# A gated cross-attention and feed-forward block on one core: the weight signs issued by ScalarE a quarter later, all values loaded ahead of the probabilities

## The reference, cut to what matters

```python
# B=4, S=512, D=1024, 64 context rows per batch, 32 query heads, 8 key/value heads, head size 128
def reference(x, ctx, mask, g_xattn, g_ffn, wq, wk, wv, wo, weight, bias, gate_w, in_scale, out_scale):
    x = x + tanh(g_xattn) * attention(layernorm(x), ctx)      # RoPE on q and k, softmax, @ wo
    h = layernorm(x).reshape(-1, 1024)
    r = softmax(h @ gate_w.T)                                 # 8 experts
    f = (h * (r @ in_scale)) @ sign(weight).T * (r @ out_scale) + bias
    return x + tanh(g_ffn) * f.reshape(x.shape)
```

## Time and profile before

| | |
|---|---|
| median of 3 runs | 1574.86 us (1572.97 to 1578.59) |
| the profiled execution | 1577.78 us |
| its span, first to last instruction | 1576.0 us |
| PE / DVE / POOL / ACT busy | 95% / 65% / 46% / 39% of the span |
| mean granted clock of PE | 0.98 |
| moved by DMA | 192.42 MB, mean 122 GB/s |

### The profile page before, as it was taken

One profiled execution on the slowest core, in us unless ns is written; L12 is line 12 of the kernel. 1 busy time (PEld: TensorE's weight loads), 2 busy tenths in 40 slices (PEclk: granted clock), 3 DMA queues, 4 the chain that ended last, 5 costly groups with the idle time before them and its releaser, 6 DMA issues. The chain is left out here.

```text
span 1576.0 us, 26125 instructions
## 1 busy us (share of the span) xinstructions
PE 1489.4 (95%) x8720; PEld 1311.5 (83%) x8720; DVE 1031.2 (65%) x2370; ACT 614.3 (39%) x1183; POOL 720.9 (46%) x586
## 2 busy tenths in 40 slices
PE   6889999999999999999999379999878999999998
PEld 5878888888888888888888279999878999987887
DVE  6737887888878888788887635455344554756553
ACT  5722222222222222222222155556555555644442
POOL 6735554555545555455554333333223333325554
PEclk9999999999999999999999689999999999999999
DMA  7832122221222212222121694444995433542221
GB/s 275 274 100 54 41 74 79 73 69 40 73 77 74 69 40 73 75 75 70 40 67 49 207 384 152 121 128 133 347 349 197 128 100 100 156 160 110 104 80 67
DMA packets 93296, 192.42 MB, mean 122 GB/s; under 512 B 9232, under 2 KB 34320, under 8 KB 93072
## 3 DMA queue, kind: packets, MB, share of 16 engines
q1 hardware_dynamic: 89344, 188.13, 37.1%
q10 hardware_dynamic: 3888, 3.48, 0.6%
HBM read 133.90 MB, written 57.67 MB: 122 GB/s over the span
## 5 line engine op out<-in xcount | busy, mean ns | idle before, releaser
L51 PE MATMUL q_ps<-x_hi,w_hi 128*128 128x512 f32 x1024 | 399.6, 390 | 3.9 <-PEq L66 3.9
L53 PE MATMUL q_ps<-x_hi,w_lo 128*128 128x512 f32 x1024 | 400.6, 391 | 0.0
L52 PE MATMUL q_ps<-x_lo,w_hi 128*128 128x512 f32 x1024 | 400.0, 391 | 0.0
L1370 DVE TENSOR_TENSOR vw_lo<-bank,vw_hi 64x256 fp32r<-64x256 f32 x512 | 215.8, 422 | 244.7 <-ACT vw_hi L1173 239.4
L1327 POOL TENSOR_TENSOR w_lo<-w_raw,w_hi 128x512 fp32r<-128x512 f32 x128 | 164.8, 1288 | 324.7 <-ACT w_hi L1165 324.7
L1026 PE MATMUL bank<-vw_hi,x_hi 128*128 128x256 f32 x1024 | 291.2, 284 | 1.4 <-DVE last_rows L1380 1.4
L1027 PE MATMUL bank<-vw_lo,x_hi 128*128 128x256 f32 x1024 | 290.4, 284 | 0.0
L1028 PE MATMUL bank<-vw_hi,x_lo 128*128 128x256 f32 x1024 | 289.9, 283 | 0.0
L595 POOL TENSOR_TENSOR q_lo<-rot,q_hi 128x512 fp32r<-128x512 f32 x128 | 165.1, 1294 | 190.4 <-ACT q_hi L561 190.3
L1173 ACT CAST vw_hi<-bank 64x256 fp32r<-64x256 f32 x512 | 188.0, 367 | 158.9 <-PE bank L53 153.8
L51 PEld LDWEIGHTS q_ps<-x_hi,w_hi 128*128 128x128 f32 x1024 | 192.7, 188 | 45.4 <-issue 4.1
(11 more groups left out here) (129 smaller groups left out, 2466.8 us busy)
## 6 DMA issues: line engine op xcount, KB each, us to landing
w_raw<-in_wo SPq DMA_DIRECT2D x128, 256.0 KB, 2.7
w_raw<-in_wq SPq DMA_DIRECT2D x32, 512.0 KB, 5.2
probs_scratch<-pt_hi SPq DMA_DIRECT2D x64, 256.0 KB, 2.5
probs_scratch<-pt_lo SPq DMA_DIRECT2D x64, 256.0 KB, 3.2
x_hi<-probs_scratch SPq DMA_DIRECT2D x32, 512.0 KB, 8.3
x_lo<-probs_scratch SPq DMA_DIRECT2D x32, 512.0 KB, 9.5
x_in<-in_x SPq DMA_DIRECT2D x16, 512.0 KB, 4.6
last_rows<-in_x SPq DMA_DIRECT2D x8, 1024.0 KB, 6.9
```

What stands on the lines that cost most here:

```text
L51: pe.matmul(out, hi, rhs_hi, start=first, stop=False, **kw)
L52: pe.matmul(out, hi, rhs_lo, start=False, stop=False, **kw)
L53: return pe.matmul(out, lo, rhs_hi, start=False, stop=last, **kw)
L1370: done = nc.vector.tensor_tensor(vw_lo[at], vw_ps[hp % VW_BANKS][b * SK:(b + 1) * SK, h, :], vw_hi[at].bitcast(F32), ALU.subtract)
```

## The change

The change has two parts.

First, in SP's stream at the start of `finish`, the values of all eight groups are loaded ahead of the first piece of probabilities; before, groups 4 to 7 were loaded between pieces of probabilities, the last ahead of piece 12.

Second, loads and stores of the signs are taken out of SP's stream and issued by ACT: blocks 0 and 1 are loaded in ACT's step 14 of quarter (0, 3), and the steps of quarter (1, 0) take the signs, store them, and load the next blocks. Even steps take a sign and load, odd steps store. Quarter (1, 0) is written out and no longer part of a loop, and the load of the first rows of the next phase (with its wait for the signs) moves to step 0 of quarter (1, 3).

```diff
--- before.py
+++ after.py
@@ over_quarters
             quarter(0, NQ - 1, (1, 0))
-            with eng.Fori(0, NQ - 1) as q:
+            quarter(1, 0, (1, 1))
+            with eng.Fori(1, NQ - 1) as q:
                 quarter(1, q, (1, q + 1))
             quarter(1, NQ - 1, None)
@@ SP
-            def load_sign_raw(k):
-                wait(sp, sign_stored[k % 2], 16 * (k // 2))
-                sp.dma_start(rows[:, k % 2], a["weight_t"][k * P:(k + 1) * P, :]).then_inc(sign_raw_in[k % 2], 16)
-
-            def store_sign(k):
-                sp.wait_ge(sign_ready, k + 1)
-                sp.dma_start(scratch["signs"][k], rows[:, k % 2]).then_inc(sign_stored[k % 2], 16)
-
-            def signs(at):
-
-                if at in (4, 6):
-                    load_sign_raw((at - 4) // 2)
-                elif 9 <= at < 9 + 2 * (KT - 2):
-                    k = (at - 9) // 2
-                    if at % 2 == 1:
-                        store_sign(k)
-                    else:
-                        load_sign_raw(k + 2)
...
@@ SP, quarter
-                    if signs_from is not None:
-                        signs(signs_from + hp)
+                    if last and hp == 0:
+                        for i in range(2):
+                            sp.wait_ge(sign_stored[i], 16 * KT // 2)
+                        sp.dma_start(x1[0], rows_block(scratch["x1"], 0)).then_inc(x1_in[0], 16)
...
-            load_values(0)
-            sp.dma_start(gate_x[:], a["g_xattn"]).then_inc(gate_in, 16)
-            sp.dma_start(gate_f[:], a["g_ffn"]).then_inc(gate_in, 16)
+            for g in range(HKV):
+                load_values(g)
+                if g == 0:
+                    sp.dma_start(gate_x[:], a["g_xattn"]).then_inc(gate_in, 16)
+                    sp.dma_start(gate_f[:], a["g_ffn"]).then_inc(gate_in, 16)
             for hp in range(HP):
-                if hp % 2 == 0 and hp // 2 + 1 < HKV:
-                    load_values(hp // 2 + 1)
...
-            quarter(0, NQ - 1, (0, NQ - 2), probs_of={hp + LAG: hp for hp in range(HP - LAG)}, signs_from=0)
-            quarter(1, 0, (0, NQ - 1), probs_of={hp - HP + LAG: hp for hp in range(HP - LAG, HP)}, signs_from=HP)
-            sp.wait_ge(x1_stored, 16 * NQ)
-            for i in range(2):
-                sp.wait_ge(sign_stored[i], 16 * KT // 2)
-            sp.dma_start(x1[0], rows_block(scratch["x1"], 0)).then_inc(x1_in[0], 16)
+            quarter(0, NQ - 1, (0, NQ - 2), probs_of={hp + LAG: hp for hp in range(HP - LAG)})
+            quarter(1, 0, (0, NQ - 1), probs_of={hp - HP + LAG: hp for hp in range(HP - LAG, HP)})
@@ ACT
+            def load_sign_raw(k):
+                wait(act, sign_stored[k % 2], 16 * (k // 2))
+                act.dma_start(rows[:, k % 2], a["weight_t"][k * P:(k + 1) * P, :]).then_inc(sign_raw_in[k % 2], 16)
+
+            def store_sign(k):
+                act.wait_ge(sign_ready, k + 1)
+                act.dma_start(scratch["signs"][k], rows[:, k % 2]).then_inc(sign_stored[k % 2], 16)
+
+            def signs(at):
+
+                if at == 0:
+                    load_sign_raw(0)
+                    load_sign_raw(1)
+                elif at % 2 == 0 and at <= 2 * KT:
+                    sign(at // 2 - 1)
+                    if at >= 4 and at // 2 < KT:
+                        load_sign_raw(at // 2)
+                elif at % 2 == 1 and 3 <= at <= 2 * KT + 1:
+                    store_sign((at - 3) // 2)
@@ ACT, quarter
-                    if pair == 0 and isinstance(q, int) and q == NQ - 1 and hp % 2 == 1:
-                        sign(hp // 2)
+                    if pair == 0 and isinstance(q, int) and q == NQ - 1 and hp == HP - 2:
+                        signs(0)
+                    if pair == 1 and isinstance(q, int) and q == 0:
+                        signs(2 + hp)
```

More of the change, by code:

```diff
@@ L894, in store_x1, with quarter @@
                 sp.dma_start(own_quarter(scratch["x1"], pair, q), x_q).then_inc(x1_stored, 16)
-            def load_sign_raw(k):
-                wait(sp, sign_stored[k % 2], 16 * (k // 2))
-                sp.dma_start(rows[:, k % 2], a["weight_t"][k * P:(k + 1) * P, :]).then_inc(sign_raw_in[k % 2], 16)
-            def store_sign(k):
-                sp.wait_ge(sign_ready, k + 1)
-                sp.dma_start(scratch["signs"][k], rows[:, k % 2]).then_inc(sign_stored[k % 2], 16)
-            def signs(at):
-                if at in (4, 6):
-                    load_sign_raw((at - 4) // 2)
-                elif 9 <= at < 9 + 2 * (KT - 2):
-                    k = (at - 9) // 2
-                    if at % 2 == 1:
-                        store_sign(k)
-                    else:
-                        load_sign_raw(k + 2)
[L914 to L917, removed]
             STORE_AT, LOAD_AT = 7, 11
-            def quarter(pair, q, earlier, probs_of=None, signs_from=None, last=False):
+            def quarter(pair, q, earlier, probs_of=None, last=False):
                 for hp in range(HP):
```

## The result

The changed kernel takes 1547.32 us (median of 4 runs, 1545.35 to 1548.59) against 1573.91 us for the kernel before (4 runs): a ratio of 0.9824, 95% interval 0.9801 to 0.9848, or 26.6 us less. The forecast was 1543.6 us, 31.3 us less, with a range of 1538 to 1560; the time lies in the range, 0.3 us above the band 1541 to 1547 that had most of the chances. Four runs of the kernel before are in this median, where the forecast had three and stood on 1574.86. The profiled execution took 1548.2 us with a span of 1546.4; from the profiled execution before (1577.78) the forecast had come to 1546.5.

What follows compares the result with a forecast made beforehand. PE was taken to be held by late values in (0, 0) and by SP's waits for sign stores around (0, 3). 8.2 - 0.7 + 24.8 - 1.0 = 31.3 us off 1574.86 gave 1543.6 us, range 1538 to 1560.

Steps and rivals of the forecast that it cites:

- What bounds the kernel: PE's waits in (0, 0), for the values, and from (0, 3) into (1, 0), where quarters lose 24.8 us.
- Signs out of SP's queue: Quarters (0, 3) and (1, 0): SP loses 16 DMAs and their waits, and the 24.8 us go whole.
- PE's lead over a late piece of wo: Quarter (0, 3): 16.5 us of lead, into which a landing of 4.7 us and 5.7 us of backlog fit.
- The reason given for it: Quarters (0, 3) and (1, 0): SP's waiting for sign stores is what is lost; 8 MB also move to a freer quarter.
- The bytes as a rival: Quarter (0, 3): mixed reads and writes limited to 347 GB/s; up to 12.4 us lost, 1556 us; chance 0.09.
- The same on ACT: Quarter (1, 0): ACT issues signs and waits for stores landing in 4 to 5 us; costs PE 1 us.
- the 5 that I had named as the limit: Sign of being right: ACT's waits for `rows` or for a store sum to less than 5 us.
- Values first: Quarter (0, 0): PE's wait and half-rate clock go, 8.2 us, less 0.7 for delayed pieces: net 7.5 us.
- The delay of what follows: Quarter (0, 0): pieces of wo behind the values come later, so PE slips by 0 to 1 us, taken as 0.7.
- values in the way: Rival, quarter (0, 0): early wo later than allowed, or PE trades waits; first part worth 0 to 4.5, 1547 to 1551; chance 0.14.
- Slower: Rival, quarter (1, 0): stores on ACT's queue land after 13.0 us; 9.6 us slower, 1584 us; chance 0.03.
- ACT at 9.2 us: Rival, quarter (1, 0): stores land after 9.2 us on ACT's queue too; 19.1 us lost, 1562 us; chance 0.06.

Runs made afterwards that it cites:

- The cross: Four kernels, values as before: signs in SP's queue, quarter (0, 3) 1574.2 us (kernel before), (1, 0) 1554.0; signs issued by ACT, (0, 3) 1564.7, (1, 0) 1551.9.
- the second profile: The changed kernel run again without any edit, for another profile and more times: 1547.13 us, ratio 0.9829 to the kernel before.

## Why the prediction was right, and what was off

*What bounds the kernel.* Right. All of the gain comes from the two places named; the other quarters of the changed kernel from (0, 1) to (1, 2) stay at 56.9 to 57.1 us, (1, 3) at 62.5 (before 62.4), and the part after the quarters takes 169.0 us (before 168.7).

*Signs out of SP's queue: 24.8 us.* The size is right: 23.0 us in the profiles (138.9 to 115.9), 22.2 in the times of this part alone. PE's lead over a late piece of wo, worked out as 16.5 us, held: with landings of up to 12.3 us (0, 3) runs at full rate, with landings of up to 18.8, median 16.7 (signs by ACT in the old quarter), it does not. The engines carried 397 to 404 GB/s, above the 384 taken from the earlier trace rows, so the backlog was smaller than thought. That writing out a quarter costs nothing was right, too (57.07 and 57.06 us with the signs six steps later).

*The reason given for it* was half right. "What the rows show to be lost is SP's waiting" is contradicted: with the signs in SP's queue a quarter later, SP waits 35.9 us instead of 34.8 and PE loses 1.4 us; with the signs by ACT in the old quarter SP waits for none and 13.7 us stay lost. What the move removes is 8.4 MB from a quarter that is already full, and a wait that only costs in such a quarter. That the 24.8 us came out nearly whole is luck as far as the reason goes: the change moves both the quarter and the queue, so its time could not tell them apart. The cross shows most of the gain to be the quarter's; the queue's share is 9.5 us where the engines are full and within the spread of the runs where they are not. The Trainium skill's "Issuing engines are not separate DMA queues" ("DMA: Bandwidth & Descriptors") says that a second issuer brings no bandwidth. The traces agree: at most 408 GB/s with both issuing at full engines, 404 with SP alone. The 9.5 us of the queue are not against it: before, the engines moved only 338 to 347.

*The bytes as a rival.* For (0, 3) of the changed kernel it was rightly dismissed, since the quarter lost nothing. But the same mechanism is what the signs by ACT in the old quarter show, with 13.7 us lost. Its 347 GB/s for reads and writes mixed was no limit of the mix: with ACT as the issuer the same mix ran at 399 to 408. The Trainium skill's 358 GB/s between HBM and on-chip memory (same page, "Where 436 GB/s comes from") is exceeded by rows of 397 to 408, and the measurement decides.

*The same on ACT: 1.0 us.* It cost 1.9 us (58.89 against 57.0). The stores landed after 3.8 to 8.3 us, median 4.9 (I took 4 to 5, plus 1 or 2 for the first blocks), ACT did wait for them, and PE did wait once. With the wait that the view gives to PE, ACT's waits for stores and weight blocks sum to some 3.4 + 3.0 + 0.4 = 6.8 us, more than the 5 that I had named as the limit. With the stores given twice the time the loss stays, and with the signs six steps later it goes. So the place of the loss is shown: the first blocks of signs meet the tail of SP's backlog of (0, 3), as the step had said. What it had not said is that wo on SP's queue would suffer too. Which of the late transfers costs PE its 1.1 to 1.6 us stays open. In the changed kernel the last wait of ACT ahead of PE's is one for a store (1.8 us, in the second profile 2.5), after one for a piece of wo (1.3 and 3.3); with the stores at once it is one for a weight block (1.2), after 3.2 for a piece of wo. "Always behind a piece of wo that is late", in the expectation for the signs six steps later, said more than the rows do.

*Values first: 7.5 us.* This is the term that was most mis-sized. Of the missing 4.7 us (31.3 against 26.6) it makes up 2.9: it gives 4.6 us on top of the other part. Another 1.6 are the signs', which alone gave 22.2 instead of 24.8 - 1.0 = 23.8. "Together 5.6 + 2.6 = 8.2" was read from one execution, at the upper end. In five profiles with the old code of (0, 0) the quarter took 70.0, 67.8, 67.9, 68.7 and 67.6 us, mean 68.4, after waits of 5.6, 4.0, 4.0, 4.9 and 3.9 us. The clock fell to a granted 0.50 in all five, but in three of them only some matmuls after the wait. In five with the values first it took 62.8, 63.0, 64.1, 64.0 and 64.6, mean 63.7. That is 4.7 us, not 7.5; the times say 2.3 (0.8 to 5.5) before the other part is made and 4.6 after it (1551.92 to 1547.32), and why they differ stays open. The delay of what follows, taken as 0.7, is 1.4 us: three profiles with the split count took 62.2, 63.1 and 61.8, mean 62.3. PE's waits say the same, 1.0, 0.5, 2.3, 1.7 and 1.6 + 0.7 us. The place was the predicted one, `vw_lo` ahead of the product of step 4 (in one profile of step 5 too).

*What it made of the sum.* From profile to profile the forecast was off by 1.7 us (1546.5 against 1548.2), since this term was measured against the very execution that it came from. The execution profiled nearest to the median (1574.24) waited 3.9 us, not 5.6, so subtracting the profile's price from the median took too much. The time of 1547.32 lies where "values in the way" put it (1547 to 1551, a first part worth 0 to 4.5), not in the band of the forecast. Of that rival's mechanism 0.7 us came true, a delay of 1.4 instead of 0.7; the larger part is that the wait cost less to begin with.

*Slower, and ACT at 9.2 us:* the landing stayed under the 11.4 us from which "slower" decides, 8.3 at most, with a median of 4.9 against the other rival's 9.2. Even beside full engines, in the old quarter, ACT's stores took 7.2 us and 9.2 at most.

## What to carry to other kernels

When a transfer stalls a kernel, first ask which stretch has room for its bytes, and only then which queue issues it: here the stretch gave 20 us in one queue and 13 in the other, the queue 9.5 where the engines were full and 2 where they were not. The total of the waits in an issuing queue is no price: 34.8 us of them went with a loss of 24.8, 35.9 with one of 1.4. Before transfers are reordered to end a wait, look at what the semaphore counts: one count for four groups made PE wait six steps early, and splitting it did at least as much as moving the loads. And a term that rests on one stall should be read from more than one execution, the more so if the clock falls behind it.

## What the runs showed of the hardware

Beside full DMA engines, a 512 KB store issued from ACT's queue, with little in it, landed in 7.2 us against 9.3 us from the queue of the probabilities; the pieces of wo on SP's queue then landed in 16.7 us against 6.8 before (issues of 1105 to 1165), when SP's own waits for the stores held its issues back. Reads of the probabilities and wo ran at 397 to 404 GB/s over 20 us and longer, and a mix with a store of signs every two steps at 399 to 408 when ACT issued the signs. With SP waiting for its own stores the same mix reached 338 to 357, with the engines busy 0.97 to 1.01 of the time against 1.03; so the busy share hardly told the two apart. After waits of 3.9 to 5.6 us PE's granted clock fell to 0.50 each time, but not at the same moment: after 3.9 and 4.0 us the next matmul still took 0.39 us, after 4.9 and 5.6 us 0.58.
